# L1 attention: every block of probabilities in seven heads turned by VectorE and moved through DRAM

## The reference, cut to what matters

```python
q = (query @ Wq + bq).reshape(B, L, NKV, G, HDIM)   # B = 8, L = 128, NKV = 8, G = 4, HDIM = 128
k_, v_ = jnp.split(kv @ Wkv + bkv, 2, axis=-1)
scores = jnp.einsum('blkgd,bmkd->bkglm', q, k) * scale
attn = jax.nn.softmax(scores, axis=-1)
o = jnp.einsum('bkglm,bmkd->blkgd', attn, v).reshape(B, L, NHEAD * HDIM)
x = x + (o @ Wo + bo)
```

## Time and profile before

| | us |
|---|---|
| median of 3 runs | 1121.05 (1119.25 to 1121.1) |
| the profiled execution | 1119.5 |
| its span, first to last instruction | 1117.7 |
| PE (tensor engine) busy | 1086.7, 97% of the span |
| DVE busy | 553.4, 50% |
| ACT busy | 532.9, 48% |
| POOL busy | 377.9, 34% |
| the hardware DMA queue | 15.0% of 16 engines' span |
| granted clock of the tensor engine, mean | 0.996 |

### The profile page before, as it was taken

One profiled execution on the slowest core, in us unless ns is written; L12 is line 12 of the kernel. 1 busy time (PEld: TensorE's weight loads), 2 busy tenths in 40 slices (PEclk: granted clock), 3 DMA queues, 4 the chain that ended last, 5 costly groups with the idle time before them and its releaser, 6 DMA issues.

```text
span 1117.7 us, 14762 instructions
## 1 busy us (share of the span) xinstructions
PE 1086.7 (97%) x5246; PEld 882.7 (79%) x5246; DVE 553.4 (50%) x1018; ACT 532.9 (48%) x1478; POOL 377.9 (34%) x260
## 2 busy tenths in 40 slices
PE   5999999999999999999999999999999999999997
PEld 4888888887877688877888888888888888888775
DVE  4465356347477443385534435345254353543654
ACT  5475367257478332456525436244262451733641
POOL 3053034024253453476503306024051240512441
PEclk9999999999999999999999999999999999999999
DMA  8111001010000221102121121120211202111002
GB/s 247 29 45 32 1 29 29 1 42 15 1 19 1 104 95 38 38 1 76 39 97 54 38 75 38 58 93 31 82 38 52 98 19 94 38 47 50 8 10 76
DMA packets 41998, 55.22 MB, mean 49 GB/s; under 512 B 20484, under 2 KB 32004, under 8 KB 39268
## 3 DMA queue, kind: packets, MB, share of 16 engines
q1 hardware_dynamic: 41956, 54.67, 15.0%
HBM read 44.69 MB, written 5.77 MB: 45 GB/s over the span
## 4 chain that ended last, share of the span: by engine, by line
PE 89%; ACT 5%; DVE 4%; issue 1%; POOL 1%; DMA 0%; SPq 0%; ACTq 0%; DVEq 0%
PE work L630 15%; PE work L631 14%; PE work L632 14%; PE work L689 8%; PE yb L630 5%; PE yb L632 5%; PE yb L631 5%; PE pt L702 3%; PE ov L630 3%; PE ov L632 3%; PE ov L631 3%; PE pt L632 3%; PE pt L631 3%; PE pt L630 3%; ACT prob L1163 2%; DVE oT_lo L1713 1%
## 5 line engine op out<-in xcount | busy, mean ns | idle before, releaser
L1390 POOL TENSOR_TENSOR prob<-prob,exp_rcp 128x512 f32<-128x512 f32 (+1 forms) x96 | 127.2, 1325 | 528.3 <-DVE exp_rcp L1642 528.3
L1163 ACT ACTIVATE prob<-work,neg_max 128x128 f32<-128x128 f32 (+1 forms) x384 | 149.1, 407 | 65.1 <-DVE neg_max L1667 64.9
L630 PE MATMUL work<-xT_hi,q_hi 128*128 128x512 f32 x416 | 168.1, 404 | 0.4 <-DVE xT_lo L1749 0.4
L632 PE MATMUL work<-xT_hi,q_lo 128*128 128x512 f32 x416 | 164.4, 395 | 0.0
L631 PE MATMUL work<-xT_lo,q_hi 128*128 128x512 f32 x416 | 164.4, 395 | 0.0
L689 PE MATMUL work<-kT,qT 128*128 128x128 f32 (+1 forms) x704 | 112.9, 303 | 0.1
L689 PEld LDWEIGHTS work<-kT,qT 128*128 128x128 f32 (+1 forms) x704 | 102.8, 191 | 11.8 <-issue 0.3
L1119 ACT ACTIVATE oT_hi<-ov 32x128 fp32r<-32x128 f32 (+2 forms) x160 | 60.2, 376 | 99.0 <-PE ov L632 96.5
L1713 DVE TENSOR_TENSOR oT_lo<-ov,oT_hi 32x128 fp32r<-32x128 f32 (+2 forms) x160 | 67.4, 421 | 74.7 <-ACT oT_hi L1119 73.3
L1667 DVE TENSOR_REDUCE neg_max<-work 128x4 f32<-128x512 f32 (+1 forms) x96 | 82.9, 863 | 39.7 <-PE work L689 37.8
L630 PE MATMUL yb<-o_hi,oT_hi 128*128 128x512 f32 x224 | 93.4, 417 | 5.1 <-DVE oT_lo L1713 5.1
(11 more groups left out here) (219 smaller groups left out, 2112.2 us busy)
## 6 DMA issues: line engine op xcount, KB each, us to landing
raw<-in_l_q SPq DMA_DIRECT2D x8, 1024.0 KB, 5.5
raw<-in_l_o SPq DMA_DIRECT2D x8, 1024.0 KB, 4.7
kv_raw<-in_l_kv SPq DMA_DIRECT2D x8, 515.0 KB, 3.4
prob<-vT SPq DMA_DIRECT2D x128, 32.0 KB, 1.8
p_bounce<-bo_bc SPq DMA_DIRECT2D x14, 256.0 KB, 2.1
prob<-p_bounce SPq DMA_DIRECT2D x56, 64.0 KB, 2.0
raw<-in_l_o SPq DMA_DIRECT2D x4, 768.0 KB, 4.2
raw<-in_l_q SPq DMA_DIRECT2D x16, 144.0 KB, 2.6
```

What stands on the lines that cost most here:

```text
L630: pe.matmul(dst, l_hi, r_hi, start=first and k == 0, stop=False)
L632: mm = pe.matmul(dst, l_lo, r_hi, start=False, stop=last and k == n - 1)
L1163: e = act.activation(prob[:, i % 2, g * L.keys:(g + 1) * L.keys], s[:, g, :], ACT.Exp, bias=neg_max[:, i % 2, g:g + 1], accum_out=exp_sum[ ...
L1390: pool.tensor_tensor(p, p, exp_rcp[:, b % 2, :].unsqueeze(2).broadcast_to([P, G, L.keys]), ALU.mult)\
```

## The change

In the first seven heads of L1 all eight blocks are turned by DVE and moved through DRAM; the tensor engine transposes none of them. The seven heads get a loop body of their own on the tensor engine, ACT and DVE (`turned_head`), while head 7 keeps the old one. Values run three steps behind the scores, so a head has 12 steps, 0 to 11, and the ahead units are done in steps 8 to 11 as 3, 2, 2 and 1. The blocks come back to the upper half of `prob`, and the moved v to the first half of `vT` instead. POOL subtracts o after normalise(1) and not after normalise(0). SP moves block 0 ahead of the load of o, and blocks 1 to 7 behind it.

```diff
+        TURN_AHEAD = (L1.ahead_all[0:3], L1.ahead_all[3:5], L1.ahead_all[5:7], L1.ahead_all[7:8])
@@ SP
+            def move_p(it, b):
+                sp.wait_ge(p_turned, it * NB + (b + 1))
+                sp.dma_start(bounce[b % 2], bo_bc[:, :]).then_inc(p_out, 16)
+                sp.wait_ge(p_out, it * (NB * 16) + 16 * (b + 1))
+                if b >= 2:
+                    sp.wait_ge(S1.pt_lo_done, it * NB + (b - 1))
+                blocks = bounce[b % 2].rearrange("(i t) (j c) -> j t i c", t=third, j=4)
+                for j in range(4):
+                    dst = prob[third * j:third * (j + 1), b % 2, HID:2 * HID].rearrange("t (i c) -> t i c", i=4)
+                    sp.dma_start(dst, blocks[j]).then_inc(p_back[b % 2], 16)
@@ SP, loop over the heads
                 load(q_raw[:, :], A["l1_q"][it], q_loaded, q_lo_done, it + L1.q0)
+                move_p(it - 1, 0)
                 load(o_raw[:, :], A["l1_o"][it], o_loaded, o_lo_done, it + L1.o0)
-                move_p(it - 1)
+                for b in range(1, NB):
+                    move_p(it - 1, b)
                 move_v(it)
@@ tensor engine
+            def turned_head(L, S, it):
+                for i in range(NB + 4):
+                    if i >= NB:
+                        for kind, u in TURN_AHEAD[i - NB]:
+                            project(L, S, it + 1, kind, u)
+                    if i == 2:
+                        project(L, S, it, "q", 6)
+                        project(L, S, it, "q", 7)
+                    if i == 3:
+                        values(L, S, it, 0)
+                    if i > 4:
+                        output(L, S, it, i - 4, (0, 1))
+                    if i < NB:
+                        scores(L, S, it, i)
+                    if i == 4:
+                        output(L, S, it, 0, (0, 1))
+                    if i == 0:
+                        pe.wait_ge(N[2].lo, NB)
+                    if i < 2:
+                        project(L, S, it, "q", 4 + i)
+                    if NB <= i:
+                        output(L, S, it, i - 4, (2, 3))
+                    if 4 <= i < NB + 3:
+                        values(L, S, it, i - 3)
+                    if 4 <= i < NB:
+                        output(L, S, it, i - 4, (2, 3))
@@ ACT
+            def back_upper(S, it, b):
+                act.wait_ge(p_back[b % 2], it * (NB * 32) + 64 * (b // 2 + 1))
+                act.activation(p_of(pT_hi[:, 0, :]), p_back_of(b), ACT.Copy).then_inc(S.pt_hi_done, 1)
...
+            def turned_head(L, S, it, next_kv, next_q):
+                for i in range(NB + 4):
+                    if i >= NB:
+                        evacuate(L, S, it + 1, *TURN_AHEAD[i - NB])
+                    if i == 2:
+                        evacuate(L, S, it, ("q", 6))
+                    if 3 <= i < NB + 3:
+                        back_upper(S, it, i - 3)
+                    if i == 3:
+                        act.wait_ge(S.act_evac, L.evacuated(it, "q", 6))
+                    if i in (3, 4, 5):
+                        next_weights(L, S, it, i, None, next_kv, next_q)
+                    if 3 <= i < NB + 3:
+                        oT_upper(L, S, it, i - 3)
+                    if i < NB:
+                        exponentials(L, S, it, i)
+                    if i == 0:
+                        evacuate(L, S, it, ("q", 4))
+                        upper_v(S, it)
+                        split_hi(o_hi, o_raw, 0, L.tiles * HID, P, o_loaded, S.scores_done, it + L.o0, it * NB + 1)\
+                            .then_inc(o_hi_done, 1)
@@ POOL, in head
-                    if b == 0:
+                    if b == (1 if L.double and norm is None else 0):
                         split_lo(o_of(L)[1], o_raw, o_of(L)[0], L.tiles * HID, P, o_hi_done, o_lo_done, it + L.o0)
@@ DVE
             def turn_p(S, it, b):
                 dve.wait_ge(S.norm_done, it * NB + (b + 1))
-                if b == TURNED[1]:
-                    dve.wait_ge(p_out, it * 32 + 16)
+                if b:
+                    dve.wait_ge(p_out, it * (NB * 16) + 16 * b)
...
+            def turned_head(L, S, it):
+                for i in range(NB + 4):
+                    if i >= 5:
+                        add_share(L, S, it, i - 5, None)
+                    if i < 3 and i:
+                        turn_p(S, it, i - 1)
+                    if i == NB:
+                        turn_p(S, it, NB - 1)
+                    if i >= NB:
+                        evacuate(L, S, it + 1, *TURN_AHEAD[i - NB])
+                    if i == 2:
+                        evacuate(L, S, it, ("q", 7))
+                    if 3 <= i < NB + 3:
+                        back_lower(S, it, i - 3)
+                    if 3 <= i < NB:
+                        turn_p(S, it, i - 1)
+                    if i < NB:
+                        negative_max(L, S, it, i, False)
+                    if 3 <= i < NB + 3:
+                        oT_lower(L, S, it, i - 3)
+                    if i < NB:
+                        dve.wait_ge(S.exp_done, it * NB + (i + 1))
+                        dve.reciprocal(exp_rcp[:, i % 2, :], exp_sum[:, i % 2, :]).then_inc(S.rcp_done, 1)
+                    if i == 0:
+                        lower_v(S, it)
+                    if i == 1:
+                        evacuate(L, S, it, ("q", 5))
+                add_share(L, S, it, NB - 1, None)
```

More of the change, by code:

```diff
@@ L692, in scores, with transpose_p @@
                 mm.then_inc(S.scores_done, 1)
-            def transpose_p(L, S, it, b, norm=None):
-                if L.double and norm is None and b in TURNED:
-                    return
+            def transpose_p(L, S, it, b):
                 pe.wait_ge(S.norm_done, it * NB + (b + 1))
@@ L1102, in split_v3, with pT_upper @@
                         .then_inc(S.v_hi_done, 1)
[L1104 to L1109, removed]
+            def pT_upper(L, S, it, b):
                 for c in range(L.sources):
-                    by_pe = NB * L.sources - (len(TURNED) if L.double else 0)
-                    act.wait_ge(S.pt_done, it * by_pe + (b * L.sources + c + 1))
+                    act.wait_ge(S.pt_done, (0 if L.double else it * NB * L.sources) + (b * L.sources + c + 1))
                     act.activation(pT_hi[:, c, :], pt[:, c, :], ACT.Copy).then_inc(S.pt_hi_done, 1)
@@ L1195, in head, with exponentials @@
                         oT_upper(L, S, it, b)
+            def back_upper(S, it, b):
+                act.wait_ge(p_back[b % 2], it * (NB * 32) + 64 * (b // 2 + 1))
+                act.activation(p_of(pT_hi[:, 0, :]), p_back_of(b), ACT.Copy).then_inc(S.pt_hi_done, 1)
+            def exponentials(L, S, it, i):
+                act.wait_ge(S.max_done, it * NB + (i + 1))
+                bank = L.score_bank(i, False)
+                for g in range(G):
+                    e = act.activation(prob[:, i % 2, g * P:(g + 1) * P], work[:, bank, g * P:(g + 1) * P], ACT.Exp,
+                                       bias=neg_max[:, i % 2, g:g + 1], accum_out=exp_sum[:, i % 2, g:g + 1])
+                e.then_inc(S.exp_done, 1)
+            def turned_head(L, S, it, next_kv, next_q):
[19 more added lines that the diff above has]
+                            .then_inc(o_hi_done, 1)
             def split_packed(it):
@@ L1235, in attention @@
                     with act.Fori(0, L.kv_heads - 1) as it:
-                        head(L, S, it, None, own_kv, own_q)
+                        turned_head(L, S, it, own_kv, own_q)
                 head(L, S, L.kv_heads - 1, norm, next_kv, next_q)
@@ L1615, in head @@
                         norm_lo(norm, 1)
-                    if L.double and norm is None and i == NB:
-                        turn_p(S, it, TURNED[1])
                     if i >= NB and norm is None:
@@ L1637, in head @@
                         add_share(L, S, it, i - 3, norm)
-                    if L.double and norm is None and i == NB - 1:
-                        turn_p(S, it, TURNED[0])
                     if i < NB:
@@ L1701, in pT_lower @@
+            def pT_lower(L, S, it, b):
                 for c in range(L.sources):
```

49 lines of the change are left out of this document (18 added, 31 removed).

## The result

| | before | after |
|---|---|---|
| median of 4 runs each, run in turn | 1120.15 | 1173.26 (1172.25 to 1174.64) |
| ratio, 95% interval | | 1.0475 (1.0456 to 1.0493) |
| span of the profiled execution | 1117.7 | 1172.8 |
| a head, heads 1 to 6 | 71.29 | 78.56 |
| the first head | 72.26 | 82.63 |

The change costs 53.1 us; 44 were forecast, with the time at 1165. The range of 1145 to 1183 holds 1173.26, the forecast's own range of 1158 to 1171 does not. A head was put at 77.6; six have 78.56, and the first, from its scores(0) at 518.81 to the next at 601.44, 82.63.

The account below looks back on a forecast made before the run. PE was taken to bound the kernel, without slack. Waits of 3.83 + 2.87 + 1.18 + 1.08 = 8.96 less 2.64 saved gave +6.3 a head, +44 in seven: 1165; own range 1158 to 1171, overall 1145 to 1183.

Parts of the forecast that it names:

- The four places: PE's waits before values(0), output(0) and values(1), and in steps 5 to 7: 3.83 + 2.87 + 1.18 + 1.08 = 8.96 a head.
- values(0): PE waits 3.83 behind scores(2), for block 2's maximum and exponentials, then block 0's copy and subtraction.
- output(0): PE waits 2.87, to 23.01 after scores(0), because the turn of block 2 waits for block 1's late write.
- values(1): PE waits 1.18 until block 1's reads have landed and its copy and subtraction are done.
- three steps without the transposes as cover: Steps 5, 6, 7: the next output's copy and subtraction take 2.46 against 2.10, losing 0.36 three times, 1.08.
- the write behind the load: On SP's queue, block 1's 256 KB write has o's 1 MB load ahead, out 5.4 behind the load's issue.
- The first rival: Block 1's write isn't held up by the load of o: net +3.8 a head, 1148; chance 0.18.
- the clock: Half rate behind the wait before values(0): values(0), scores(3), scores(4) take 2.48 more, free because they end before output(0) could start.
- a half rate that ends midway: Half rate outlasting the waits into output(0) and values(1): +2.3 a head, 1181, chance 0.20; half of that if ending midway, 1173.
- the subtraction of a turned block: On DVE, priced at 0.65 in the chains before values(0) and values(1).
- the forecast on its terms: Profiled execution of 1119.5 plus 44 in seven heads: 1163.7, against 1165 on the median's terms.
- the rival "faster": PE runs through at 4.38 a step, a head's waits all under the 2.64 saved: 1102.6; chance 0.04.

Follow-up runs that it names:

- o loaded late: Changed kernel with SP issuing the load of o behind block 3's reads, not ahead of block 1's write: 1174.69, ratio to before 1.0479.
- 14 matmuls: Changed kernel with 14 matmuls of 128 x 512 into the unused tile pt in front of values(0): 1172.19, ratio to before 1.0464.
- subtraction from PSUM: Changed kernel with a turned block's subtraction reading unused PSUM tile pt, without the permuted view, so numbers differ: 1166.03, ratio to before 1.0405.

## Why the prediction was right, and where it was off

**Right: the order on PE, and what it uncovers.** The four places that it named are those that lose, in nearly its sizes: values(0) wait 4.29 (3.83 forecast), output(0) starts at 23.11 after scores(0) (23.01), values(1) 1.12 (1.18), three steps without the transposes as cover. The load of o is issued at 15.02 (15.09). The sum came out at 1165 for 1173.26.

**Right: the write behind the load.** The forecast had it out 5.4 after the load's issue; it took 5.96. The first rival, 1148, assumed that write to be free, and it fell. Its price was wrong as well: with the write free and the order on PE as it was (o loaded late) the time is 1174.69, since half clock then holds scores(3) up for just as long, which the rival's sum left out. The Trainium skill's rule of rings emptied in order (DMA: Bandwidth & Descriptors, "Queues, rings and completion order") agrees with this row.

**Right in its size: the clock.** Half clock came behind values(0) and was gone by 626, as forecast. It doesn't stand beside the wait for output(0) but in its place; the run with the 14 matmuls shows nearly the same head with and without it (78.28 to 78.48 against 78.56). That the result, 1173.26, equals the number given for a half rate that ends midway is chance: that rival put 2.3 of half rate behind output(0), and the first three matmuls there took 0.82 (624.55 to 625.37) against 0.70, so 0.1 was paid.

**Mis-sized: the subtraction of a turned block.** The prediction took 0.65 for it, from a row of before where POOL was idle; it measured 0.98 in the mean. Along the head at 601.44: 0.67 more makes values(0) late by 0.65 (18.31 against 17.66), and the wait for the write takes that back at output(0). Behind that, values(1) is 0.34 late, the next output comes 0.1 sooner than its sum, the two steps take 5.03 and 4.93 for 4.74, and from there to the end of the head 0.27 is added: 78.6 for 77.6. In the first head the subtraction came after the normalisation, when POOL's split of q (549.71 to 552.06) had just started, and stood until its end; rows of DVE and PE:

```profile
550.07 2.54 DVE L1755 TENSOR_TENSOR pT_lo<-prob,pT_hi 128x512 fp32r<-128x512 f32 x1 [0.84 <-ACT pT_hi L1225]
```

```profile
552.66 0.55 PE L632 MATMUL ov<-pT_hi,v_hi 128*128 128x512 f32 x1 [2.30 <-DVE pT_lo L1755]
553.02 0.63 PE L633 MATMUL ov<-pT_lo,v_hi 128*128 128x512 f32 x1
```

PE waited 2.30 and went on at 0.63 a matmul. That head lost 10.4 (82.63 - 72.26) and not 6.3. In sum 6 x 0.96 + 4.1 = 9.9 of the 10.9 by which the profiled execution (1174.64, the slowest of the four) exceeds the forecast on its terms (1163.7). The rest lies outside the seven heads. In the last layer PE's matmuls from 1150.34 to 1153.74 run at half clock (0.50 from 1151 to 1153) behind a wait of 0.88 that the kernel before has too and passes at 1.00; that costs 1.5, and the first scores(0) came 0.4 sooner than before. The forecast had no term for it, and why the clock fell there is not shown. The subtraction from PSUM takes 7.2 away by the medians.

The Trainium skill has the rule that I should have weighed: SBUF — State Buffer, section "Who interferes with whom". A DVE instruction with two inputs in SBUF and a GpSimd instruction that reads SBUF exclude each other, and the one issued first keeps the port. The trace agrees on both sides, 0.98 against 0.69 on DVE and 2.85 against 2.39 on POOL.

**What became of the rival "faster".** It gave 1102.6, if all waits of a head stay under the transposes. It was dismissed rightly, since by the changed kernel's order they could not; but the work itself fits, and with another order 1101.56 is that number.

## What to carry to other kernels

Price a transfer or an engine's operation by what will run beside it in the new place, not by the row where it ran alone. Two waits in series hide each other: undoing one of them shows nothing (1174.63, 1174.69), undoing both shows 25 us, so single reversals don't clear a suspect. When work leaves the engine that sets the pace, what is gained depends on the order of the rest; here the same instructions took 1173 or 1102.

## What the runs showed of the hardware

- DVE's subtraction of two SBUF operands waits for a POOL operation on SBUF that runs already: in all 35 cases of the seven heads it ends 0.54 to 0.56 after POOL does (subtractions of 0.70 to 2.54), and without one it takes 0.69. POOL's splits that begin beside it take 2.85 for 2.39. With one of DVE's operands in PSUM neither happens (0.69 and 2.39).
- On one queue a 256 KB write 0.5 behind a 1 MB load was out after 5.35 to 5.48; alone it took 2.0.
- The same wait didn't always bring the clock down at the same place. Behind the 4.29 of the changed kernel a matmul took 0.77 in six heads; in the seventh it took 0.47, and the granted clock was 0.50 only from 1014 on, 1.3 later. Behind some 1.9 (14 matmuls) it fell to 0.50 in two of heads 1 to 6 and stayed at 1.00 in four. Through waits of 1.70, 0.58 and 1.18, one behind the other, it stayed at 1.00.
